# The last tile of a fused decoder layer: raw rows turned and scaled later, the residuals brought in by TensorE, and two pieces of work moved in the queues

## The chip, the cores and the metric

The kernel runs on 1 core of a Trainium2 chip. The metric is the device time of one execution in microseconds. The kernel before has a median of 396.46 us over 3 runs (395.39 to 398.01). The engines are named as the profile names them: PE is TensorE (PEld its weight loads), DVE is VectorE, ACT is ScalarE, POOL is GpSimd, SP is SyncE, which issues loads.

## What is computed

A decoder layer with the norm behind each residual, on x of 8 sequences of 128 tokens, 512 wide, in float32:

```python
x = _layernorm(x + _L0_attn_ref(x, ...))       # rmsnorm, mamba2, residual; rmsnorm, gated MLP 512-1792-512, residual
x = _layernorm(x + _L0_xattn_ref(x, ctx_4096)) # softmax(x ctx^T) ctx, ctx of 128 keys per sequence
x = _layernorm(x + _L0_ffn_ref(x, ...))        # x W_up^T + a rank-8 update of the one expert of 4 with the highest logit
```

where `_layernorm` subtracts the mean and divides by sqrt(var + 1e-5), over the 512 values of a row, without weights. The expert is `argmax(x gate_w^T + expert_bias)`.

## The kernel before

Everything is written out by hand, engine by engine, with counting semaphores: each engine runs its block in order, and `wait_ge(s, n)` halts all behind it on that engine. A tile is one sequence: 128 tokens on the partitions, 512 values along the row. A product of fp32 accuracy is made of three fp32r products (`three_pass`, lines 656 to 658): high by low, high by high, low by high parts, so each operand needs a high part (a copy with rounding, mostly ScalarE) and a low part (a subtraction, VectorE or GpSimd).

The program has three stages. First the mamba2 block (0 to about 132 us): input projections in the order of `IN_ORDER`, whose products `in_proj(n)` feed convolutions and, from n = 14 on, the gate z; `decays_of(b)` builds the exponents of sequence b (two kinds of bf16 products) and then transposes x and the steps of sequence b into bank 5. For b >= 1 these transposes wait for `xb_ok` of sequence b - 1, since bank 5 is one for all: ScalarE's `decay(b - 1)` copies it out (line 1147). `decays_after` says behind which projections the first two stand. Second, gate and up projections (to about 265 us), partly as Strassen products; at their end the down weights and the base weights (W_up with the gate and LoRA columns) are loaded by SP, rounded by ScalarE (`wd_high`, `bw_high`, line 1322) and their low parts made by VectorE and GpSimd.

Third, the tiles (265 us to the end). A tile t passes: `down(t)`, 14 blocks of 128 of the hidden layer, three products each into bank 0 or 1, cut into segments (`SEGS`, for the last tile `END_SEGS`) between which other tiles' pieces stand; `add_mlp` (VectorE: bank + rows, the residual), `moments(0)`, `rstd(0)` (ScalarE: log, then exp), `normed(0)`; `turn_x1` (four transposes), `copy_q`, `attend` (scores against `keyT`, loaded), `row_max`, `exp_scores`, `turn_ex`, `mix` (weights by `key`, loaded), `add_attention`, `moments(1)`, `rstd(1)`, `normed(1)`; `turn_x2`, `copy_x2` and `low_x2` (high and low part of x2), `base` (side 1 holds half of the columns with the logits and LoRA columns, 292 wide; side 0 the other 256), `choose` and `routed` (VectorE: eight small steps from logits to the masked LoRA values; line 1801 is the first, 1825 the last), `turn_z`, `copy_z`, `lora`; `add_ffn` (bank + x2, the residual, line 1842), `moments(2)`, `rstd(2)`, `normed(2)`, `store`. The moments are bn_stats and bn_aggr (lines 1789 and 1791), rstd is lines 1378 and 1380, normed is line 1796.

The tiles are staggered: while `down(t)` runs, tile t - 1 has its attention and tile t - 2 its base, with t - 3 finishing (`tail`, in a loop over pairs of tiles). For the last three tiles the order is written out on each engine behind the loop (`last = 7`); x1 and x2 of tile 7 are turned in two halves (`turn_halves`, `copy_halves`, `low_halves`). SP loads `keyT` and `key` of tile t into the place of its hidden rows once these are split. `store` is a DMA issued from ScalarE's queue, line 1384.

## Time and profile before

| | |
|---|---|
| median of 3 runs | 396.46 us (395.39 to 398.01) |
| the profiled execution | 396.79 us |
| its span, first to last instruction | 395.0 us |
| PE busy | 382.7 us, 97% |
| DVE, ACT, POOL busy | 285.1, 192.5, 152.6 us |
| mean granted PE clock | 0.996 |
| DMA, mean | 65 GB/s |

Idle time is given with what ended it. Matmuls overlap in the rows of the timeline: a row of 0.39 us can begin 0.23 us after the one before. The chain that ended last follows the work back from the last instruction and shows each step without that overlap.

### The profile page before, as it was taken

What the parts mean: (1) busy time and instruction counts of PE and PEld (TensorE: products, weight loads), DVE (VectorE), ACT (ScalarE), POOL (GpSimd) and SP (SyncE); (2) the same over time, 40 slices, a digit from 0 to 9 for tenths busy, and PEclk for the clock granted to TensorE, in tenths of its full rate; (3) what the DMA queues carried; (4) which work ended last, traced back from release to release, by engine and by line L of the source; (5) the groups of instructions that cost most, each with busy time, mean ns of one, the idle gap of its engine ahead of it and who ended that gap; (6) DMA issues with size and microseconds to landing.
All of it is one profiled execution on the core that took longest, in us unless ns stands there. A gap on an engine that the chain in (4) does not pass through costs nothing.

```text
span 395.0 us, 5385 instructions
## 1 busy us (share of the span) xinstructions
PE 382.7 (97%) x1926; PEld 311.5 (79%) x1926; DVE 285.1 (72%) x504; ACT 192.5 (49%) x388; POOL 152.6 (39%) x139
## 2 busy tenths in 40 slices
PE   7999998999999999999999999999999999999983
PEld 3878886766688998888888888887788888897863
DVE  4599981267764987979797979695666756676575
ACT  5868766876757644252424243863324144142241
POOL 6406425844599742738282837850000000000000
PEclk9999999999999999999999999999999999999998
DMA  8901110110001033120212111352110120101002
GB/s 268 319 2 54 55 53 0 54 55 0 2 0 53 3 83 133 53 78 31 95 22 95 52 56 53 124 162 87 55 54 28 54 81 27 53 29 51 27 2 80
DMA packets 11659, 25.52 MB, mean 65 GB/s; under 512 B 1681, under 2 KB 1809, under 8 KB 11634
## 3 DMA queue, kind: packets, MB, share of 16 engines
q1 hardware_dynamic: 10480, 23.10, 18.3%
q10 hardware_dynamic: 1154, 2.10, 1.4%
q8 instruction: 14, 0.23, 0.3%
q14 instruction: 11, 0.09, 0.1%
HBM read 23.10 MB, written 2.10 MB: 64 GB/s over the span
## 4 chain that ended last, share of the span: by engine, by line
PE 71%; DVE 15%; POOL 5%; issue 3%; ACT 3%; DMA 1%; SPq 0%; DVEq 0%; ACTq 0%
PE bank_first L656 8%; PE bank_first L658 8%; PE bank_first L657 8%; PE bank L656 7%; PE bank L657 7%; PE bank L658 7%; DVE big L1546 5%; PE bank_last L656 5%; PE bank_last L657 5%; PE bank_last L658 5%; PE bank L923 2%; PE bank L934 2%; PE bank_last L727 2%; POOL rows L545 1%; PE bank_last L736 1%
## 5 line engine op out<-in xcount | busy, mean ns | idle before, releaser
L656 PE MATMUL bank_first<-sets,station 128*128 128x512 f32 (+1 forms) x172 | 69.9, 406 | 0.1
L656 PE MATMUL bank<-sets,station 128*128 128x512 f32 (+1 forms) x180 | 67.5, 375 | 0.3 <-POOL station L488 0.3
L657 PE MATMUL bank<-sets,station 128*128 128x512 f32 (+1 forms) x180 | 66.1, 367 | 0.0
L658 PE MATMUL bank<-sets,station 128*128 128x512 f32 (+1 forms) x180 | 66.0, 367 | 0.0
L658 PE MATMUL bank_first<-sets,station 128*128 128x512 f32 (+1 forms) x172 | 65.6, 381 | 0.0
L657 PE MATMUL bank_first<-sets,station 128*128 128x512 f32 (+1 forms) x172 | 65.4, 380 | 0.0
L656 PEld LDWEIGHTS bank<-sets,station 128*128 128x128 f32 x180 | 34.3, 190 | 6.8 <-POOL station L488 0.7
L656 PEld LDWEIGHTS bank_first<-sets,station 128*128 128x128 f32 x172 | 32.4, 189 | 8.4 <-issue 2.8
L657 PEld LDWEIGHTS bank<-sets,station 128*128 128x128 f32 x180 | 34.3, 190 | 5.8 <-issue 0.5
L658 PEld LDWEIGHTS bank<-sets,station 128*128 128x128 f32 x180 | 34.2, 190 | 5.5
L657 PEld LDWEIGHTS bank_first<-sets,station 128*128 128x128 f32 x172 | 32.4, 188 | 6.8 <-issue 1.7
L658 PEld LDWEIGHTS bank_first<-sets,station 128*128 128x128 f32 x172 | 32.3, 188 | 6.4
L608 POOL TENSOR_TENSOR big<-tmp,side_f 128x512 f32<-128x512 f32 x17 | 26.5, 1573 | 24.7 <-DVE side_f L1672 24.7
L1378 ACT ACTIVATE small<-small 128x1 f32<-128x1 f32 x24 | 7.1, 295 | 45.7 <-DVE small L1791 45.7
L656 PE MATMUL bank_last<-sets,station 128*128 128x512 f32 (+1 forms) x76 | 28.0, 368 | 0.0
L658 PE MATMUL bank_last<-sets,station 128*128 128x512 f32 (+1 forms) x76 | 27.9, 367 | 0.0
L657 PE MATMUL bank_last<-sets,station 128*128 128x512 f32 (+1 forms) x76 | 27.9, 367 | 0.0
L488 POOL TENSOR_TENSOR station<-raw,station 128x1024 fp32r<-128x1024 f32 x7 | 16.7, 2390 | 26.7 <-ACT station L1056 26.7
L1656 DVE TENSOR_TENSOR station<-raw,station 128x512 fp32r<-128x512 f32 (+1 forms) x24 | 19.0, 832 | 6.1 <-ACT station L1281 6.1
L1281 ACT ACTIVATE station<-raw 128x512 fp32r<-128x512 f32 x12 | 7.5, 625 | 29.8 <-PE bank L658 17.9
L1666 DVE TENSOR_TENSOR station<-side_f,station 128x512 fp32r<-128x512 f32 x24 | 19.5, 814 | 2.1 <-ACT station L1289 2.1
L1546 DVE SCALAR_TENSOR_TENSOR big<-bank,cw,big 128x508 f32<-128x508 f32 (+2 forms) x27 | 19.7, 738 | 0.9 <-ACT big L1129 0.3
(250 smaller groups left out, 867.4 us busy)
## 6 DMA issues: line engine op xcount, KB each, us to landing
raw<-wstream SPq DMA_DIRECT2D x31, 512.0 KB, 3.7
rows<-x SPq DMA_DIRECT2D x8, 256.0 KB, 5.1
big<-ctxT SPq DMA_DIRECT2D x8, 256.0 KB, 2.6
big<-ctx SPq DMA_DIRECT2D x8, 256.0 KB, 3.0
out<-tmp ACTq DMA_DIRECT2D x8, 256.0 KB, 2.0
big<-ln_w SPq DMA_DIRECT2D x1, 256.0 KB, 5.9
big<-lora_b SPq DMA_DIRECT2D x3, 64.0 KB, 5.6
ga<-gate_lora SPq DMA_DIRECT2D x1, 72.0 KB, 5.8
```

Source lines behind the costliest of these rows:

```text
L488: pool.tensor_tensor(dst, raw[:, raw_slot(n), :], hi.bitcast(F32), ALU.subtract).then_inc(w_lo, 1)
L608: pool.tensor_tensor(hid_block(m, hf), blocks(sg[:, k, :]), blocks(value), ALU.mult).then_inc(up_ok, 1)
L656: pe.matmul(ps, a_hi, b_lo, start=first, stop=False)
L657: pe.matmul(ps, a_hi, b_hi, start=False, stop=False)
L658: return pe.matmul(ps, a_lo, b_hi, start=False, stop=last)
L727: pe.matmul(bank[6][:, :], bT[:, tok(b)], cT[:, :, tok(b)], start=True, stop=True).then_inc(s1_done, 1)
L923: mm = pe.matmul(bank[4][:, 0:P], qT[:, bass.ts(c, P)], blocks(keyT)[:, c, :], start=(c == 0), stop=(c == DC - 1))
L934: pe.matmul(bank[5][:, :], exT, key, start=True, stop=True).then_inc(pv_ps, 1)
L1281: act.activation(groupS[:, buf, 0, 0:D], raw[:, raw_slot(n), 0:D], ACT.Copy).then_inc(g_hi, 1)
L1546: v.scalar_tensor_tensor(out=dst[:, :, s:L], in0=src[:, :, 0:L - s], scalar=cw[:, m, 3 - s:4 - s], in1=dst[:, :, s:L], op0=ALU.mult, op1=A ...
L1656: v.tensor_tensor(groupS[:, buf, 1, lo:hi], src, groupS[:, buf, 0, lo:hi].bitcast(F32), ALU.subtract) \
L1666: v.tensor_tensor(groupS[:, buf, 1, q], sums[:, bass.ts(k, D)], groupS[:, buf, 0, q].bitcast(F32), ALU.subtract).then_inc(g_lo, 1)
```

## The change

1. `decays_of(1)` stands one projection later on PE (`decays_after`).
2. GpSimd adds the identity to the four diagonal blocks of the base weights before they are rounded, so that base products contain x2 itself. `add_ffn` goes away for all tiles: moments and norm of the third layernorm read the PSUM banks. It also makes an fp32r identity and the high and low part of tile 7's rows; PE adds two products of these to tile 7's down sum (`add_rows`), so `add_mlp(7)` goes away.
3. For tile 7, ScalarE subtracts the mean of each key row from the key (`center_key`), PE turns it (`turn_key`), ScalarE copies it (`copy_keyT`); the load of `keyT` of tile 7 goes away. With centred keys the mean of x1 adds nothing to the scores that differs between keys, so the raw row is turned (`copy_raw`, `turn_halves`) and 1/std enters as the scale of the exponential (`raw_row_max`, `exp_raw_scores`). Mixing with centred keys shifts a row by a constant, which the next layernorm takes out.
4. x2 of tile 7 is turned before its norm as well: logits are scaled in `choose` (`scale=`), and the last rstd takes the scale in (`rstd_raw`, `rstd_scaled`).
5. The order behind the loop is new: base and lora of tile 5 stand in the middle of the last down projection, those of tile 6 around tile 7's attention, in other banks. Banks are named in four pairs, in the same places.

PE around the second `decays_of` (L710, L712 and L720, L721 are its rows, the rows of L656 to L658 are projections). Before:

```order
L658 MATMUL bank<-sets,station 128x512
L710 MATMUL bank_first<-big,identb 128x512 [waits rows_ok]
L712 MATMUL bank_first<-cs_56,tmp 128x128 x4
L720 MATMUL bank<-ident,big 128x128 [waits xb_ok,cv_done]
L721 MATMUL bank<-ident,big 128x128
L656 MATMUL bank_last<-sets,station 128x512 [waits z_done,hT_lo,w_lo]
L657 MATMUL bank_last<-sets,station 128x512
```

After (710, 712, 720, 721 are 730, 732, 740, 741 there, and 656 to 658 are 676 to 678):

```order
L677 MATMUL bank_last<-sets,station 128x512
L678 MATMUL bank_last<-sets,station 128x512
L730 MATMUL bank_first<-big,identb 128x512 [waits rows_ok]
L732 MATMUL bank_first<-cs_56,tmp 128x128 x4
L740 MATMUL bank_third<-ident,big 128x128 [waits xb_ok,cv_done]
L741 MATMUL bank_third<-ident,big 128x128
L676 MATMUL bank_second<-sets,station 128x512 [waits z_done,hT_lo,w_lo]
```

The decays now stand behind the projection into bank_last.

PE around the turned exponential and the mix of tile 7 (L929 and L934 before, L968 and L973 after). Before:

```order
L929 MATMUL bank<-ident,tmp 128x128 [waits ex_ok]
L656 MATMUL bank_first<-side,rawS 128x292 [waits x2_lo]
L657 MATMUL bank_first<-side,rawS 128x292
L658 MATMUL bank_first<-side,rawS 128x292
L934 MATMUL bank<-big,tmp 128x512 [waits exT_ok]
L656 MATMUL bank_first<-side,rawS 128x292
L657 MATMUL bank_first<-side,rawS 128x292
L658 MATMUL bank_first<-side,rawS 128x292
```

After:

```order
L968 MATMUL bank_third<-ident,tmp 128x128 [waits ex_ok]
L676 MATMUL bank_second<-side,rawS 128x256
L677 MATMUL bank_second<-side,rawS 128x256
L678 MATMUL bank_second<-side,rawS 128x256
L973 MATMUL bank_third<-big,tmp 128x512 [waits exT_ok]
L676 MATMUL bank_second<-side,rawS 128x256
L677 MATMUL bank_second<-side,rawS 128x256
L678 MATMUL bank_second<-side,rawS 128x256
L676 MATMUL bank_second<-side,rawS 128x256
L677 MATMUL bank_second<-side,rawS 128x256
L678 MATMUL bank_second<-side,rawS 128x256
L948 MATMUL bank_first<-ident,tmp 128x128 [waits ln2_u]
```

Before, one chunk of tile 6's base stands ahead of the mix and seven behind it; after, six stand ahead of it (the last two of them shown) and two behind, with the first transposes of the raw x2 (L948) next.

VectorE from tile 7's attention residual on. Before (L1866 is the residual, L1789, L1791 and L1796 moments and norm, L1801 to L1825 the routing of tile 6, L1842 would follow):

```order
L1866 SCALAR_TENSOR_TENSOR tmp<-bank,small,tmp 128x512 [waits pv_ps,rinv_ok]
L1789 BN_STATS tmp<-tmp 128x6 [waits ln2_u]
L1791 BN_AGGR small<-tmp 128x2 [waits ln2_st]
L1801 TENSOR_TENSOR tmp<-bank_first,eb 128x4 [waits route_ps]
L1803 TENSOR_REDUCE small<-tmp 128x1 [waits lg_step]
L1805 SCALAR_TENSOR_TENSOR tmp<-tmp,small,codes 128x4 [waits lg_step]
L1796 TENSOR_SCALAR tmp<-tmp,small 128x512 [waits ln2_rs]
L1811 TENSOR_REDUCE small<-tmp 128x1 [waits lg_step]
L1813 TENSOR_SCALAR tmp<-tmp,small 128x4 [waits lg_step]
L1817 TENSOR_TENSOR tmp<-bank_first,tmp 128x32 [waits lg_step]
L1822 CAST tmp<-tmp 128x2x32 [waits z_step]
L1825 TENSOR_TENSOR tmp<-tmp 128x32 [waits z_step]
```

After (L2000 is the residual in halves, L1924 to L1938 the rest of tile 6's routing, L1958 the low halves, L1887 the moments of tile 7):

```order
L2000 SCALAR_TENSOR_TENSOR tmp<-bank_third,small,tmp 128x256 [waits ln1_out,pv_ps,rinv_ok]
L2000 SCALAR_TENSOR_TENSOR tmp<-bank_third,small,tmp 128x256
L1924 TENSOR_REDUCE small<-tmp 128x1 [waits lg_step]
L1926 TENSOR_SCALAR tmp<-tmp,small 128x4 [waits lg_step]
L1930 TENSOR_TENSOR tmp<-bank_second,tmp 128x32 [waits lg_step]
L1935 CAST tmp<-tmp 128x2x32 [waits z_step]
L1938 TENSOR_TENSOR tmp<-tmp 128x32 [waits z_step]
L1958 TENSOR_TENSOR rawS<-bank_first,rawS 128x256 [waits x2_hi] x2
L1887 BN_STATS tmp<-tmp 128x6 [waits ln2_u]
L1889 BN_AGGR small<-tmp 128x2 [waits ln2_st]
L1903 TENSOR_SCALAR tmp<-bank_last,small 128x512 [waits ln3_rs,stored]
L1913 SCALAR_TENSOR_TENSOR tmp<-bank_third,small,eb 128x4 [waits ln2_rs,route_ps]
```

The routing's last five steps now stand between the residual and the low halves, and the norm of tile 7 is gone from between them.

ScalarE at the store of tile 5 (DMA; L1378 and L1380 before, L1462 and L1464 after are rstd(1) of tile 7). Before:

```order
L1378 ACTIVATE small<-small 128x1 [waits ln2_mv]
L1380 ACTIVATE small<-small 128x1 [waits ln2_log]
L1398 ACTIVATE rawS<-bank 128x256 [waits x2_ps] x2
L1409 ACTIVATE zmT<-bank 96x128 [waits zmT_ps]
L1384 DMA out<-tmp 128x512 [waits ln3_out]
L1409 ACTIVATE zmT<-bank 96x128 [waits zmT_ps]
L1378 ACTIVATE small<-small 128x1 [waits ln3_mv]
L1380 ACTIVATE small<-small 128x1 [waits ln3_log]
```

After:

```order
L1493 ACTIVATE rawS<-bank_first 128x256 [waits x2_ps] x2
L1504 ACTIVATE zmT<-bank_first 96x128 [waits zmT_ps]
L1479 DMA out<-tmp 128x512 [waits ln3_out]
L1462 ACTIVATE small<-small 128x1 [waits ln2_mv]
L1464 ACTIVATE small<-small 128x1 [waits ln2_log]
L1465 ACTIVATE small<-small 128x1
L1466 ACTIVATE small<-small 128x1
```

That rstd stood ahead of the copies of x2 and of the store; it now stands behind the store.

The diff, cut to what the prediction speaks of:

```diff
-END_SEGS = ((0, 8), (8, 9), (9, 10), (10, 11), (11, 14))
+END_SEGS = ((0, 8), (8, 9), (9, 10), (10, 11), (11, 13), (13, 14))
...
+                if t < B - 1:
+                    sp.dma_start(keyT, ctxT[t]).then_inc(ctx_in[t % 2], 16)
...
+            for c in range(DC):
+                n = base_load(c // 2)
+                pool.wait_ge(raw_in[raw_slot(n)], landed(n))
+                diagonal = raw[:, raw_slot(n), bass.ds((c % 2) * D + c * P, P)]
+                pool.tensor_tensor(diagonal, diagonal, ident[:, :], ALU.add).then_inc(eye_ok, 1)
+            pool.wait_ge(wd_lo, NM // 2 - len(POOL_WD))
+            pool.wait_ge(bw_lo, 2)
+            pool.wait_ge(hx_ok, B)
+            pool.tensor_copy(identS, ident[:, :]).then_inc(eye_ok, 1)
+            pool.tensor_copy(rowsS[:, 0, :], rows[:, B - 1, :]).then_inc(eye_ok, 1)
+            pool.wait_ge(eye_ok, DC + 2)
+            pool.tensor_tensor(rowsS[:, 1, :], rows[:, B - 1, :], rowsS[:, 0, :].bitcast(F32), ALU.subtract).then_inc(eye_ok, 1)
...
-            decays_after = {N_DVE_IP + 3: 0, N_DVE_IP + 4: 1}
+            decays_after = {N_DVE_IP + 3: 0, N_DVE_IP + 5: 1}
...
+            def add_rows():
+                pe.wait_ge(eye_ok, DC + 3)
+                for part in range(2):
+                    pe.matmul(bank[1][:, :], identS, rowsS[:, part, :], start=False, stop=False)
+            def turn_key():
+                pe.wait_ge(key_ok, 2)
+                pe.wait_ge(ln_u[0], B - 1)
+                _, key = context(B - 1)
                 for c in range(DC):
+                    mm = pe.transpose(bank[0][:, bass.ts(c, P)], key[:, bass.ts(c, P)], ident[:, :])
+                mm.then_inc(key_ok, 1)
...
+            add_rows()
+            turn_key()
             turn_x1(last - 1)
             turn_x2(last - 2, 1)
             down(last, 1, 1, False, END_SEGS)
...
             turn_ex(last - 1)
             down(last, 1, 3, False, END_SEGS)
             mix(last - 1)
-            down(last, 1, 4, False, END_SEGS)
             base(last - 2, 1)
             base(last - 2, 0)
             turn_x2(last - 1, 0)
-            turn_halves(last, u1, ln_out[0], (2, 0), q_ps)
+            down(last, 1, 4, False, END_SEGS)
+            pe.wait_ge(ln_u[1], last)
+            turn_z(last - 2, bk=5)
+            down(last, 1, 5, False, END_SEGS)
+            lora(last - 2)
+            base(last - 1, 1, range(1), pair=2)
+            turn_halves(u1, ln_u[0], B, (0, 2), q_ps)
+            base(last - 1, 1, range(1, 2), pair=2)
             attend(last, 1, halves=True)
-            turn_z(last - 2, bk=1)
-            lora(last - 2)
+            base(last - 1, 1, range(2, DC), pair=2)
+            base(last - 1, 0, range(1), pair=2)
             turn_ex(last)
-            base(last - 1, 1, range(1), pair=0)
+            base(last - 1, 0, range(1, 2), pair=2)
             mix(last)
-            base(last - 1, 1, range(1, DC), pair=0)
-            base(last - 1, 0, pair=0)
-            turn_halves(last, u2[:, 1, :], ln_out[1], (3, 5), x2_ps)
-            turn_z(last - 1)
-            base(last, 1, range(2), halves=True, free=last - 1)
-            lora(last - 1, pair=0)
-            base(last, 1, range(2, DC), halves=True)
-            base(last, 0)
-            turn_z(last)
-            lora(last)
+            base(last - 1, 0, range(2, DC), pair=2)
+            turn_halves(u2[:, 1, :], ln_u[1], B, (0, 1), x2_ps)
+            base(last, 1, range(2), pair=4, halves=True)
+            turn_z(last - 1, bk=0)
+            base(last, 1, range(2, DC), pair=4, halves=True)
+            lora(last - 1, pair=2)
+            base(last, 0, pair=4)
+            turn_z(last, bk=1)
+            lora(last, pair=4)
...
+                act.wait_ge(eye_ok, 2 * (i + 1))
...
+            def center_key():
+                act.wait_ge(ctx_in[1], 16 * (B - 1))
+                _, key = context(B - 1)
+                act.activation(x1_last, key, ACT.Copy, scale=-1.0 / D, accum_out=key_mean).then_inc(key_ok, 1)
+                act.wait_ge(key_ok, 1)
+                act.activation(key, key, ACT.Identity, bias=key_mean, scale=1.0).then_inc(key_ok, 1)
...
+            def copy_raw():
+                act.wait_ge(down_ps, B)
+                act.wait_ge(ln_u[1], B - 1)
+                for i in range(2):
+                    q = bass.ts(i, 2 * P)
+                    act.activation(u1[:, q], bank[1][:, q], ACT.Copy).then_inc(ln_u[0], 1)
...
+            def rstd_raw(t):
+                act.wait_ge(ln_mv[1], t + 1)
+                act.activation(log2_last, mv[:, 1, 1:2], ACT.Ln, bias=epsc[:, :]).then_inc(ln_log[1], 1)
+                act.wait_ge(ln_log[1], t + 1)
+                act.activation(lrs[:, 1:2], log2_last, ACT.Exp, scale=-0.5).then_inc(ln_rs[1], 1)
+                act.activation(half2_last, log2_last, ACT.Copy, scale=-0.5).then_inc(ln_rs[1], 1)
+                act.activation(r2sq_last, log2_last, ACT.Exp, scale=-1.0).then_inc(ln_rs[1], 1)
+            def rstd_scaled(t, slot):
+                r = lrs[:, slot:slot + 1]
+                act.wait_ge(ln_mv[2], t + 1)
+                act.wait_ge(ln_rs[1], t + 3)
+                act.activation(r, mv[:, slot, 1:2], ACT.Ln, bias=epsc[:, :], scale=r2sq_last).then_inc(ln_log[2], 1)
+                act.wait_ge(ln_log[2], t + 1)
+                act.activation(r, r, ACT.Exp, bias=half2_last, scale=-0.5).then_inc(ln_rs[2], 1)
...
+            center_key()
             copy_q(last - 1)
             copy_x2(last - 2)
             store(last - 3)
             exp_scores(last - 1)
             rstd(1, last - 1)
+            copy_keyT()
+            copy_x2(last - 1)
+            copy_z(last - 2, bk=5)
+            copy_raw()
+            copy_halves(last, qT, q_ps, (0, 2), q_ok)
             rstd(0, last)
-            copy_halves(last, qT, q_ps, (2, 0), q_ok)
-            copy_x2(last - 1)
-            copy_z(last - 2, bk=1)
-            exp_scores(last)
+            exp_raw_scores(last)
             rstd(2, last - 2)
-            rstd(1, last)
-            copy_halves(last, x2S[:, 0, :], x2_ps, (3, 5), x2_hi)
-            copy_z(last - 1)
+            copy_halves(last, x2S[:, 0, :], x2_ps, (0, 1), x2_hi)
+            copy_z(last - 1, bk=0)
             store(last - 2)
-            copy_z(last)
+            rstd_raw(last)
+            copy_z(last, bk=1)
             rstd(2, last - 1)
-            rstd(2, last, slot=0)
+            rstd_scaled(last, 0)
             store(last - 1, u1)
             store(last, u_last)
...
+            def ffn_normed(t, u=u3, pair=6, slot=None, stored_tiles=None):
+                normed(2, t, in_two(u), slot, src=pairs[pair // 2][:, :, 0:D // 2])
+            def normed(i, t, u, slot=None, src=None):
                 k = i if slot is None else slot
                 v.wait_ge(ln_rs[i], t + 1)
-                v.tensor_scalar(u, u, mv[:, k, 0:1], lrs[:, k:k + 1], ALU.subtract, ALU.mult).then_inc(ln_out[i], 1)
+                v.tensor_scalar(u, u if src is None else src, mv[:, k, 0:1], lrs[:, k:k + 1], ALU.subtract, ALU.mult).then_inc(ln_out[i], 1)
...
+            def raw_row_max(t):
+                v.wait_ge(sc_ps, t + 1)
+                v.tensor_reduce(sm[:, 0:1], bank[4][:, 0:P], AX.X, ALU.max, negate=True).then_inc(mx_ok, 1)
+                v.wait_ge(mx_ok, t + 1)
+                v.wait_ge(ln_rs[0], t + 1)
+                v.tensor_tensor(bias_last, sm[:, 0:1], lrs[:, 0:1], ALU.mult).then_inc(mx_ok, 1)
+            def add_attention_halves(t):
+                v.wait_ge(ex_ok, t + 1)
+                v.reciprocal(sm[:, 2:3], sm[:, 1:2]).then_inc(rinv_ok, 1)
+                v.wait_ge(rinv_ok, t + 1)
+                v.wait_ge(pv_ps, t + 1)
+                v.wait_ge(ln_out[0], t + 1)
+                for i in range(2):
+                    q = bass.ts(i, 2 * P)
+                    v.scalar_tensor_tensor(out=u2[:, 1, q], in0=bank[5][:, q], scalar=sm[:, 2:3], in1=x1_last[:, q],
+                                           op0=ALU.mult, op1=ALU.add).then_inc(ln_u[1], 1)
...
-            add_mlp(last, 1)
-            moments(0, last, u1)
+            choose(last - 2)
             normed(1, last - 1, u2[:, 0, :])
-            normed(0, last, u1)
-            route(last - 2)
-            row_max(last)
+            routed(last - 2)
             low_x2(last - 1)
-            add_ffn(last - 2, 1, stored_tiles=last - 2)
-            moments(2, last - 2, u3)
-            add_attention(last, 1)
-            moments(1, last, u2[:, 1, :])
-            choose(last - 1, bk=1)
-            normed(1, last, u2[:, 1, :])
-            routed(last - 1, bk=1)
+            raw_moments(last)
+            ffn_moments(last - 2)
+            raw_row_max(last)
+            normed(0, last, x1_last, src=u1)
+            choose(last - 1, bk=3)
+            add_attention_halves(last)
+            routed(last - 1, bk=3)
             low_halves(last)
-            add_ffn(last - 1, 0, u=u1, pair=0)
-            normed(2, last - 2, u3)
-            route(last)
-            moments(2, last - 1, u1)
-            add_ffn(last, 1, u=u_last)
-            moments(2, last, u_last, slot=0)
-            normed(2, last - 1, u1)
-            normed(2, last, u_last, slot=0)
+            moments(1, last, u2[:, 1, :], value=B + 1)
+            ffn_normed(last - 2, stored_tiles=last - 2)
+            choose(last, bk=5, scale=lrs[:, 1:2])
+            routed(last, bk=5)
+            ffn_moments(last - 1, pair=2)
+            ffn_moments(last, pair=4, slot=0)
+            ffn_normed(last - 1, u=u1, pair=2)
+            ffn_normed(last, u=u_last, pair=4, slot=0)
```

## Rows read from the trace of the kernel before

**Rows 1.** Busy us (xcount) by stretch: PE, PEld, DVE, ACT, POOL; clock, DMA, GB/s

```profile
383.00:395.00 12.00, 5.29 (x34) 4.26 (x34) 7.37 (x23) 2.20 (x8) 0.00 (x0) 0.87 0.17 66
sum 395.00, PE 382.68 PEld 311.46 DVE 285.10 ACT 192.53 POOL 152.61; mean PE 38.27 PEld 31.15 DVE 28.51 ACT 19.25 POOL 15.26
```

**Rows 2.** Waits of TensorE, whole span: who waited for whom, us, times, longest

```profile
PE bank L720 <- ACT big L1147: 1.2, 1, 1.2
```

**Rows 3.** Timeline, 66 to 110 us: start, us, engine, line, op, names, count, [idle before]

```profile
66.69 0.39 PE L712 MATMUL bank_first<-cs,tmp 128*128 128x128 bf16 x4
...
68.30 0.30 PE L720 MATMUL bank<-ident,big 128*128 128x128 f32 x1 [1.22 <-ACT big L1147]
...
67.85 0.31 ACT L1147 ACTIVATE big<-bank 128x164 f32<-128x164 f32 x1
...
109.28 1.30 POOL L541 TENSOR_TENSOR big<-big 128x512 f32<-128x512 f32 x1 [2.57 <-DVE big L1582]
```

**Rows 4.** Timeline, 261 to 274 us: base weights, and tile 0's first norm

```profile
261.97 1.24 POOL L635 CAST side<-ga 128x144 fp32r<-128x144 f32 x1 [1.17 <-DVE big L1678]
263.29 0.55 POOL L637 TENSOR_TENSOR side<-ga,side 128x144 fp32r<-128x144 f32 x1
...
264.80 1.04 ACT L1322 ACTIVATE side<-raw 128x1024 fp32r<-128x1024 f32 x1
266.78 1.07 ACT L1322 ACTIVATE side<-raw 128x1024 fp32r<-128x1024 f32 x1 [0.94 <-DMA raw<-wstream]
...
272.40 0.55 DVE L1796 TENSOR_SCALAR tmp<-tmp,small 128x512 f32<-128x512 f32 x1 [0.60 <-ACT small L1380]
...
273.70 0.60 PE L905 MATMUL bank<-ident,tmp 128*128 128x128 f32 x4
```

**Rows 5.** Timeline, 128 us: GpSimd and VectorE side by side

```profile
128.56 2.40 POOL L563 TENSOR_TENSOR sets<-sets_f,sets 128x1024 fp32r<-128x1024 f32 x1
...
128.71 2.80 DVE L1625 SCALAR_TENSOR_TENSOR tmp<-tmp,rst,big 128x512 f32<-128x512 f32 x1 [3.01 <-POOL rows L545]
```

**Rows 6.** Chain that ended last, 359 to 373 us: start, us, what

```profile
359.14 0.23 PE bank_first L656
...
364.61 0.44 PE bank L905 x4
...
366.17 0.91 PE bank L923 x8
...
368.97 0.86 PE bank L934 x2
...
372.32 0.14 PE bank_last L656
```

**Rows 7.** Timeline, 363 us to the end: the last tile's chain

```profile
363.57 0.29 ACT L1378 ACTIVATE small<-small 128x1 f32<-128x1 f32 x1 [1.01 <-DVE small L1791]
...
378.11 0.33 PE L929 MATMUL bank<-ident,tmp 128*128 128x128 f32 x1
...
378.81 1.13 PE L934 MATMUL bank<-big,tmp 128*128 128x512 f32 x2
...
380.04 0.75 DVE L1866 SCALAR_TENSOR_TENSOR tmp<-bank,small,tmp 128x512 f32<-128x512 f32 x1
...
383.82 0.76 DVE L1853 TENSOR_TENSOR rawS<-bank,rawS 128x256 fp32r<-128x256 f32 x2
...
386.72 0.15 DVE L1801 TENSOR_TENSOR tmp<-bank_last,eb 128x4 f32<-128x4 f32 x1
...
388.27 0.19 DVE L1825 TENSOR_TENSOR tmp<-tmp 128x32 fp32r<-128x32 f32 x1
...
389.75 0.69 DVE L1842 TENSOR_TENSOR tmp<-bank_last,tmp 128x512 f32<-128x512 f32 x1 [0.46 <-PE bank_last L970]
...
391.98 0.55 DVE L1796 TENSOR_SCALAR tmp<-tmp,small 128x512 f32<-128x512 f32 x1 [0.17 <-ACT small L1380]
...
386.84 0.35 ACTq L1384 DMA_DIRECT2D out<-tmp  x1
```

92 lines of the change are left out of this document (60 added, 32 removed).

## The prediction

> **What bounds the kernel now.** I read the page first, then the busy times by stretch. TensorE is busy 382.68 us of 395.00 [rows 1], so only its waits and its queue's contents can move the time; VectorE and ScalarE matter where they keep TensorE waiting, and after its last product. In the list of waits TensorE's longest is 1.2 us, one time, at L720, on ScalarE's L1147 [rows 2]. Then the timeline, at the two places. Around 68 us TensorE has the decays of sequence 1 in its queue, and their transposes need xb_ok, which ScalarE gives only after a table load and the copy at 67.85 [rows 3]. From 383 to 395 us TensorE is busy 5.29 of 12.00 us [rows 1]: there the kernel is a chain of VectorE, ScalarE and short TensorE pieces, and what counts there is VectorE's order.
>
> I write all times on the clock of the trace of before, and subtract the gain of the first edit at the end.
>
> **Edit 1, decays of sequence 1 one projection later.** Before, TensorE ends the row-sum products of the decays at 66.69+0.39 and then stands still 1.22 us until 68.30 [rows 3]. After, the 12 products of the next projection, which before follow the transposes, come first. Twelve products of 0.23 us [rows 6] are 2.8 us, so they run from 66.5 to 69.3, the decays' five bf16 products reach to 69.7 and the transposes start at 69.7: xb_ok has been there since 67.85+0.31 = 68.16. ScalarE comes to the transposed steps later still, behind the exponentials of sequence 0 and two rounding copies of weights. Gain: 1.22 us. Is it kept? What follows is TensorE's own queue until the last VectorE-bound stretch. GpSimd is dense between 109 and 131 us, but its start there waits 2.57 us for VectorE, which follows TensorE [rows 3], so that stretch moves along. I take the whole 1.22; the bounds are 0 (absorbed there) and 1.22.
>
> **Edit 2, identity added to the base weights on GpSimd, rows of tile 7 split.** Four additions of 128x128 come ahead of ScalarE's two copies of the base weights. ScalarE makes these at 264.80 and, released by the DMA, at 266.78 [rows 4]. GpSimd's last work before ends at 263.84 [rows 4]. A 128x128 addition is not in the trace; from a CAST of 128x144, 1.24 us, and the subtraction of the same size, 0.55 us [rows 4], I put it at 0.4 to 1.2. The first pair is then ready by 264.6 to 266.2, the second 0.8 to 2.4 us after 266.78. Behind their readers VectorE has the first tile's residual and moments; its norm is at 272.40 and TensorE turns it at 273.70 [rows 4], so there are 0.75 us of slack (273.70 less 272.95). Behind them GpSimd splits identity and rows: three more pieces, during just these VectorE pieces. What this does is shown at another place: GpSimd's L563 runs from 128.56 for 2.40 us, and VectorE's L1625, started at 128.71, takes 2.80 us [rows 5], where the same operation on the same shape takes 0.75 alone, at 380.04 [rows 7]. It ended only after GpSimd did. The Trainium skill, "GPSIMD Engine Reference", section 1 (Specifications), says that the two engines share their SBUF interfaces, and that a VectorE instruction with two SBUF inputs or in a two-port mode contends; these two rows agree. Cost on TensorE: 0 if the collisions stay inside the 0.75 us; at worst the norm (0.55 us) begins when GpSimd ends. With 0.3 + 1.24 + 2.50 us for the three pieces from 270.9 on (2.50: each as slow as the 2.40 of L563), that is 274.9, the norm ends at 275.5, and TensorE loses 1.8 us. I take 0.3, nearer the lower end, since it needs several collisions in a row to use up the slack. The body of the loop loses one addition of 0.67 to 0.69 us per tile on VectorE (L1842), worth nothing: TensorE is busy there throughout, and VectorE isn't waited for. If the norm out of PSUM were slower, the base products of the next tile would wait for it; they stand behind the down products of a segment and the attention, so I count nothing.
>
> **Edit 3, the last tile.** TensorE first, up to the second product of the attention of tile 7 (mix). From the start of the last down projection at 359.14 its queue holds: 42 products of 0.23 (9.6), two for the rows (0.46), five groups of four transposes of 0.44 (2.2), two attends of 0.91 (1.8), one mix of 0.86, 12 base products of 0.14 and 12 of about 0.12 for tile 5 (3.0; an estimate, 0.14 times 256/292), 12 and 6 for tile 6 (2.3), two lora products and three single transposes (0.6), and the wait for the exponential that it has before (0.4): 21.2 us, ending at 380.4 [rows 6]. From turning the exponential to the mix it is 0.70 us before (378.11 to 378.81), and the two short base products fill only half of it: mix(7) at 380.65, against 378.81 [rows 7], 1.84 us later. I find no wait on ScalarE or VectorE that ends later than TensorE's own queue there. The closest is the centred key: the reciprocal root of tile 4 starts at 363.57 [rows 7], 0.7 earlier without the residual addition, takes 0.5, and two passes over the key of 0.8 and 0.6 (estimates from the 0.55 to 0.75 of whole rows here) end at 364.9, when TensorE comes to it at 365.1.
>
> From there VectorE's order decides. Before: the residual of the attention at 380.04, moments, norm, four transposes, low half of x2 at 383.82 [rows 7], base of tile 7 half a microsecond behind. After: 1.23 us behind the mix, so 381.9; two halves of 0.42 each (an estimate: a little over half of 0.75); then the routing of tile 6, still open, five of the eight small steps that go from 386.72 to 388.46 before, so 1.1 us [rows 7], to 383.85; then the low halves. So base(7) starts when it did: what the raw rows save in front (moments and norm, 1.42 us, and the wait for ScalarE) is spent on the later mix and on the routing. Its side 1 ends at 386.15.
>
> Now the choice of tile 7's expert. It needs ln_rs[1], since x2 was turned raw. VectorE after the low halves (384.6): moments of tile 7 (0.69, 0.18), then the norm of tile 5 out of PSUM, to 386.06. On ScalarE the store of tile 5 stands ahead of rstd_raw and waits for that norm; an issue takes 0.35 us [rows 7]. So rstd_raw starts at 386.4, and the pair of functions with its handovers is 0.60 us [rows 4]: VectorE may choose at 387.05, before it was 386.72 [rows 7]. Loss 0.33, with 0.06 for the scaled add 0.39; nothing if the issue hides (then 0.04).
>
> Behind it: transposed z, its copy, lora: 0.39 later, so VectorE goes on at 390.14 instead of 389.75 [rows 7]. The residual addition of 0.69 [rows 7] is gone: moments at 390.14, ScalarE 0.60 behind, norms from 391.65. The last norm reads PSUM. A tensor_scalar from SBUF takes 0.55, a tensor_tensor from PSUM 0.69 [rows 4, 7]; a tensor_scalar from PSUM is not in the trace, so 0.55 to 0.69; I take 0.68. The Trainium skill, "VectorE: DVE Perf Modes", "Why PSUM operands drop a tier", says that fp32 tensor_scalar runs two elements a cycle only from SBUF; by it the PSUM form has the longer time, and by the SBUF row the end would be 0.14 earlier. So the last norm ends at 392.33; before it is 391.98+0.55 = 392.53 [rows 7]. The two stores behind it keep their 2.5 us to 395.0. Gain of the tail: 0.20. Bounds: issue hidden and norms at 0.55, twice on the path: 0.35+0.28 more, 0.85. A late key, slower halves or transposes: each moves mix(7) and all behind it, down to a loss of 0.5.
>
> **Sum.** 1.22 - 0.3 + 0.2 = 1.1 us off the profiled execution's 396.79 gives 395.7. That execution is 0.33 over the median of 396.46, so I predict **395.4 us**. A change of under 1% (4 us) is about what a measurement of this kernel can't tell from none.
>
> **Rivals.**
> - *Forecast* (1.22 kept, small collision, tail about even): 395.4, chance 0.45.
> - *The tail pays more*: the store's issue hides and the norms cost no more from PSUM. For it: the 0.35 us are the issue's, and nothing in the trace shows how soon a function can start behind one; against: ScalarE's block is in order, and the store waits for the very norm. 0.65 us more, and no collision in edit 2 another 0.3: 394.4. Chance 0.22.
> - *The first edit isn't kept*: GpSimd between 109 and 131 us absorbs it. Against: its 2.57 us wait ahead. Then 1.22 is missing: 396.6. Chance 0.10.
> - *GpSimd holds VectorE at the start of the tiles* (the other side): the place is VectorE's norm at 272.40; the price is 1.8 us at the bound above instead of 0.3, so 396.8, slower than before; it decides from a stall of 1.4 us on TensorE's first transposes of x1, where the two other terms are used up. For it: 2.80 us at 128.71; against: the slack of 0.75 and that the pieces must line up. Chance 0.15. The Trainium skill's line on the shared interfaces ("GPSIMD Engine Reference", section 1) speaks for this one.
> - *Something in the new order waits that I don't see* (two us either way): 0.08.
>
> **How the numbers follow.** The cases reach from 394.4 to 396.8; with the bounds of the tail (0.65 better, 0.7 worse) and some half us for a median of single runs that lie between 395.39 and 398.01, 8 in 10 lie between 393.6 and 397.2. None of the named cases reaches 4 us: faster by over 1% 0.03, within 1% 0.94, slower by over 1% 0.03.
>
> **What would show it.** In the trace after: no wait of TensorE at the decays' transposes near 69 us (edit 1; a wait anywhere in 70 to 135 that is not there now would be where it went). TensorE's first transposes of x1 in tile 0 without a wait: edit 2 hidden; a wait on the norm there, beside a GpSimd cast: the slow rival. The distance from the start of the last down projection to mix(7), 21.5 us; VectorE's low halves right behind the last step of tile 6's routing; the choice of tile 7 waiting for ScalarE rather than for the base products; the last norm 0.68 us. I would be wrong if TensorE waited for the centred key, if the ScalarE functions of the tail brought a table load, or if the halves took as long as whole pieces.

## The result, and the profile after

The changed kernel takes 397.63 us (median of 20 runs, 397.13 to 399.39) where the kernel before takes 396.20 (20 runs, 395.31 to 398.01): a ratio of 1.0034 with a 95% interval of 1.0023 to 1.0045. It is slower by 1.35 us (0.9 to 1.8), where 395.4 was predicted, a gain of 1.1.

TensorE is as busy as before, 382.83 us; its waits have moved. One stretch of the changed kernel (columns as in [rows 1]: window, its length, then TensorE, weight loads, VectorE, ScalarE, GpSimd busy, clock, DMA):

```profile
250.00:275.00 25.00, 23.36 (x104) 18.39 (x103) 20.32 (x22) 14.91 (x17) 18.91 (x14) 1.00 0.43 144
```

TensorE has waits of 1.64 us between 250 and 275, where before it had none that the profile lists, and GpSimd's work there has grown from 11.76 to 18.91 us. In the loop behind it, 275 to 359, TensorE is busy for 84.00 of 84.00 us in both kernels.

The traces differ by up to 2.4 us in when TensorE comes to the first product of the attention of sequence 0 (61.44 to 63.83), so I compare distances between fixed places of the order of work, not times from the start. The places are, in the changed kernel's timeline (start, length, engine, line): the first product of the attention of sequence 0, the turn of the normed rows of sequence 7, the first transposes of x1 of tile 0, and VectorE's last norm.

```profile
62.02 1.02 PE L747 MATMUL bank_last<-big 128*128 128x512 f32 x2
...
130.22 0.66 PE L778 MATMUL bank_last<-ident,tmp 128*128 128x128 f32 x4 [0.52 <-DVE tmp L1723]
...
274.03 0.66 PE L925 MATMUL bank_second<-ident,tmp 128*128 128x128 f32 x4 [1.02 <-DVE tmp L1903]
...
392.63 0.81 DVE L1903 TENSOR_SCALAR tmp<-bank_third,small 128x512 f32<-128x512 f32 x1
```

In the kernel before the first two stand here (the other two are in [rows 4] at 273.70, and the last norm ends at 392.53, of which [rows 7] shows the start):

```profile
62.86 1.02 PE L727 MATMUL bank_last<-big 128*128 128x512 f32 x2
...
131.57 0.66 PE L758 MATMUL bank_last<-ident,tmp 128*128 128x128 f32 x4 [0.52 <-DVE tmp L1625]
```

The differences between these starts, and to the end of the last norm, in us; the same four places in every kernel of this study:

| kernel | start | middle | loop and tail | sum | ratio to before, timed |
|---|---|---|---|---|---|
| before | 68.71 | 142.13 | 118.83 | 329.67 | 1 |
| changed | 68.20 | 143.81 | 119.41 | 331.42 | 1.0034 [1.0023, 1.0045] |
| changed, again | 68.18 | 143.82 | 119.40 | 331.40 | 1.0041 [1.0028, 1.0054] |
| b_decay | 67.94 | 142.14 | 118.90 | 328.98 | 0.9983 [0.9974, 0.9992] |
| b_hold | 67.82 | 142.12 | 118.93 | 328.87 | 0.9982 [0.9969, 0.9994] |
| a_noadd | 68.20 | 142.10 | 119.31 | 329.61 | 1.0006 [0.9993, 1.0020] |
| a_late | 68.20 | 142.10 | 119.29 | 329.59 | 0.9999 [0.9987, 1.0011] |
| a_pair | 67.96 | 143.19 | 119.31 | 330.46 | 1.0019 [1.0001, 1.0038] |
| a_half | 68.21 | 143.42 | 119.39 | 331.02 | 1.0054 [1.0033, 1.0074] |
| a_store | 68.23 | 143.81 | 118.58 | 330.62 | 1.0034 [1.0021, 1.0047] |
| a_late_store | 68.21 | 142.10 | 118.47 | 328.78 | 0.9973 [0.9962, 0.9983] |
| a_best | 67.58 | 142.10 | 118.46 | 328.14 | 0.9971 [0.9957, 0.9986] |

So the three edits gave -0.51, +1.68 and +0.58 us, +1.75 in all, where -1.22, +0.3 and -0.2 had been predicted. The distances repeat to 0.03 us between the two profiled executions of the changed kernel. The start, though, has two outcomes 0.24 us apart in kernels with the same edits (68.20 and 67.96; 67.82 and 67.58); b_hold's section shows them. The timed intervals reach 0.4 to 0.8 us to either side, so a smaller step rests on the traces.

**Start.** The wait in the decays [rows 3] is gone: TensorE's L732, L740 and the product behind them follow each other. But 11 us later there is a new one. GpSimd, VectorE and TensorE in the changed kernel's timeline:

```profile
68.59 0.39 PE L732 MATMUL bank_first<-cs,tmp 128*128 128x128 bf16 x4
68.82 0.28 PE L740 MATMUL bank_third<-ident,big 128*128 128x128 f32 x1
...
76.96 2.37 POOL L495 TENSOR_TENSOR station<-raw,station 128x1024 fp32r<-128x1024 f32 x1
78.20 1.68 DVE L1694 TENSOR_TENSOR station<-tmp,station 128x512 fp32r<-128x512 f32 x1 [1.02 <-ACT station L1203]
80.02 0.47 PE L676 MATMUL bank_second<-side,station 128*128 128x512 f32 x1 [0.52 <-DVE station L1694]
```

In the kernel before, the same two subtractions did not meet:

```profile
77.84 2.36 POOL L488 TENSOR_TENSOR station<-raw,station 128x1024 fp32r<-128x1024 f32 x1
80.41 0.69 DVE L1596 TENSOR_TENSOR station<-tmp,station 128x512 fp32r<-128x512 f32 x1 [1.02 <-ACT station L1156]
```

Once the wait is gone, VectorE comes to it while GpSimd still has its 128x1024 subtraction, and takes 1.68 us for what takes 0.69: TensorE waits 0.52 for it.

**Middle.** The four identity adds, one by one, and what VectorE and ScalarE did beside them, in the changed kernel's timeline:

```profile
262.44 1.44 POOL L651 TENSOR_TENSOR raw<-raw,ident 128x128 f32<-128x128 f32 x1
263.84 1.44 POOL L651 TENSOR_TENSOR raw<-raw,ident 128x128 f32<-128x128 f32 x1
265.24 2.23 POOL L651 TENSOR_TENSOR raw<-raw,ident 128x128 f32<-128x128 f32 x1
267.43 1.44 POOL L651 TENSOR_TENSOR raw<-raw,ident 128x128 f32<-128x128 f32 x1
...
262.05 1.52 DVE L1781 TENSOR_TENSOR sets<-raw,sets 128x1024 fp32r<-128x1024 f32 x1
263.49 1.47 DVE L1781 TENSOR_TENSOR sets<-raw,sets 128x1024 fp32r<-128x1024 f32 x1
264.88 2.28 DVE L1881 TENSOR_TENSOR station<-big,station 128x1792 fp32r<-128x1792 f32 x1
267.08 1.47 DVE L1787 TENSOR_TENSOR side<-raw,side 128x1024 fp32r<-128x1024 f32 x1
...
265.37 1.06 ACT L1370 ACTIVATE side<-raw 128x1024 fp32r<-128x1024 f32 x1 [1.83 <-POOL raw L651]
268.96 1.06 ACT L1370 ACTIVATE side<-raw 128x1024 fp32r<-128x1024 f32 x1 [2.53 <-POOL raw L651]
```

In the kernel before, VectorE's same instructions stood there without an add beside them:

```profile
263.41 2.65 DVE L1683 TENSOR_TENSOR sets<-raw,sets 128x1024 fp32r<-128x1024 f32 x2
265.98 2.01 DVE L1783 TENSOR_TENSOR station<-big,station 128x1792 fp32r<-128x1792 f32 x1
```

Each add lasts almost as long as the VectorE instruction beside it: 1.44 beside 1.47 to 1.52, 2.23 beside 2.28. ScalarE's second copy of the base weights, at 266.78 before [rows 4], starts at 268.96, though by the second of the places above (130.22 for 131.57) the kernel is 1.35 us ahead there: 3.5 us late. TensorE pays twice: here, for a VectorE that is itself slower (2.28 us for 2.01), and at the first transposes of x1 (274.03 above, 1.02 us) for the norm behind the late copy.

```profile
267.31 0.47 PE L676 MATMUL bank_first<-sets,station 128*128 128x512 f32 x1 [0.62 <-DVE station L1881]
```

**Tail.** From the second product of tile 7's attention to the end, in the changed kernel's timeline:

```profile
381.47 1.12 PE L973 MATMUL bank_third<-big,tmp 128*128 128x512 f32 x2
382.69 0.88 DVE L2000 SCALAR_TENSOR_TENSOR tmp<-bank_third,small,tmp 128x256 f32<-128x256 f32 x2 [1.50 <-issue]
384.49 0.75 DVE L1958 TENSOR_TENSOR rawS<-bank_first,rawS 128x256 fp32r<-128x256 f32 x2
...
385.98 0.80 DVE L1903 TENSOR_SCALAR tmp<-bank_last,small 128x512 f32<-128x512 f32 x1
386.81 0.35 ACTq L1479 DMA_DIRECT2D out<-tmp  x1
387.20 0.29 ACT L1462 ACTIVATE small<-small 128x1 f32<-128x1 f32 x1 [0.75 <-DVE tmp L1903]
387.83 0.22 DVE L1913 SCALAR_TENSOR_TENSOR tmp<-bank_third,small,eb 128x4 f32<-128x4 f32 x1 [1.06 <-ACT small L1465]
...
389.69 0.33 PE L1004 MATMUL bank_first<-ident,tmp 128*128 128x128 f32 x1 [1.08 <-DVE tmp L1938]
...
391.88 0.39 ACT L1473 ACTIVATE small<-small 128x1 f32<-128x1 f32 x1 [0.85 <-DVE small L1889]
```

It is the chain that the prediction drew: VectorE norms tile 5 out of PSUM, only then does ScalarE issue the store, only then does it take the logarithm for tile 7 (387.20), and VectorE, with nothing else to do for 1.06 us, waits to choose tile 7's expert.

### The profile page after: what moved, and what is told of

Same layout as the page of the kernel before. It is cut to its first block and busy times, and to the rows that moved or that the text cites. A ratio compares the mean times of both kernels' runs of the same rounds, so it can differ in the third digit from the quotient of the medians.

```text
span 395.9 us, 5408 instructions
## 1 busy us (share of the span) xinstructions
PE 382.8 (97%) x1928; PEld 311.2 (79%) x1932; DVE 282.7 (71%) x497; ACT 195.8 (49%) x396; POOL 161.4 (41%) x146
## 5 line engine op out<-in xcount | busy, mean ns | idle before, releaser
L676 PE MATMUL bank_second<-sets,station 128*128 128x512 f32 (+1 forms) x96 | 35.6, 370 | 0.0
L678 PE MATMUL bank_second<-sets,station 128*128 128x512 f32 (+1 forms) x96 | 34.8, 363 | 0.0
L677 PE MATMUL bank_second<-sets,station 128*128 128x512 f32 (+1 forms) x96 | 34.8, 363 | 0.0
L676 PE MATMUL bank_third<-sets,station 128*128 128x512 f32 (+1 forms) x84 | 31.7, 378 | 0.4 <-POOL station L495 0.4
L678 PE MATMUL bank_third<-sets,station 128*128 128x512 f32 (+1 forms) x84 | 31.0, 369 | 0.0
L677 PE MATMUL bank_third<-sets,station 128*128 128x512 f32 (+1 forms) x84 | 31.0, 369 | 0.0
L676 PEld LDWEIGHTS bank_second<-sets,station 128*128 128x128 f32 x96 | 18.1, 189 | 3.4 <-issue 0.5
```

Of the source, the lines that this page charges most:

```text
L676: pe.matmul(ps, a_hi, b_lo, start=first, stop=False)
L677: pe.matmul(ps, a_hi, b_hi, start=False, stop=False)
L678: return pe.matmul(ps, a_lo, b_hi, start=False, stop=last)
```

## Experiments

The theories after the result: (1) the middle's loss is the four adds, each held by a VectorE instruction; (2) rivals to it: an add of this size costs 1.4 us by itself, or its rate by the element is lower beside VectorE; (3) the tail's loss is the store ahead of ScalarE's three steps; (4) the first edit, alone, keeps its 1.2 us.

**b_decay: the first edit alone.** On the kernel before:

```diff
-            decays_after = {N_DVE_IP + 3: 0, N_DVE_IP + 4: 1}
+            decays_after = {N_DVE_IP + 3: 0, N_DVE_IP + 5: 1}
```

> The kernel before with the decays of sequence 1 one input product later and nothing else. Theory (edit 1 is kept and the other two edits cost): 1.2 us faster than before, near 395.0, with TensorE free of the 1.22 us wait at 68.3 and every later instruction about 1.3 us earlier. Rival (the gain of edit 1 is given back where GpSimd and VectorE meet, whatever the identity adds do): between 0 and 0.4 us faster, TensorE busy in 250 to 275 as little as in the changed kernel (23.4 of 25).

0.9983 of before, 0.7 us; by the trace 0.69 (0.77 at the start). That is neither theory's number. Two of TensorE's waits from 61 to 131 us say where the rest went:

```profile
PE bank L656 <- DVE station L1596: 0.5, 1, 0.5
PE bank L656 <- POOL station L488: 0.2, 1, 0.2
```

The second stands in the kernel before too (0.31 us there); the first is new and is the 0.5 that comes off 1.22. Theory 4 falls.

**b_hold: keep the two subtractions apart.** b_decay, and on GpSimd:

```diff
+            pool.wait_ge(y_lo, 1)
             lo_part(GU_CHUNK, ringS[:, 0, 1, :], ringS[:, 0, 0, :])
```

> The kernel before with the decays of sequence 1 later, and with one wait more: GpSimd's subtraction for the first loop weight (128x1024, 2.36 us at 76.91) starts only when VectorE's subtraction for y of sequence 0 is done. Theory (edit 1 loses 0.5 us at 80 because these two instructions now overlap and VectorE's takes 1.67 us instead of 0.69): VectorE's takes 0.69 again, TensorE's wait of 0.52 at 80 is gone, and the kernel is 1.0 to 1.3 us faster than before, near 394.5 where before has 395.75. Rival (TensorE would wait at 80 anyway, for ScalarE or for the chain of sequence 1): the time of edit 1 alone, 0.5 to 0.8 us faster than before, with a wait of 0.3 or more left near 80.

VectorE's subtraction takes 0.69 us again and the wait at 80 is gone, so the overlap was its cause. The time doesn't tell what that is worth: 0.9982 against b_decay's 0.9983, with intervals of 0.4 us and more to either side. By the table the start gains only 0.12 us on b_decay, but that pair isn't like with like. About 117 us in, VectorE and GpSimd come to their next instructions together, and one of them is held. Here are the changed kernel and then a_pair, whose program is the same up to there:

```profile
116.60 0.74 DVE L1723 SCALAR_TENSOR_TENSOR tmp<-tmp,rst,big 128x512 f32<-128x512 f32 x1
116.64 1.30 POOL L561 TENSOR_TENSOR sets_f<-sets_f 128x256 f32<-128x256 f32 x1
...
117.66 1.33 DVE L1724 SCALAR_TENSOR_TENSOR tmp<-tmp,rst,big 128x512 f32<-128x512 f32 x1
117.70 0.74 POOL L561 TENSOR_TENSOR sets_f<-sets_f 128x256 f32<-128x256 f32 x1
```

Where GpSimd is held, TensorE's next wait for it is 0.43 us (at 123.25); where VectorE is held, 0.19 us (at 124.05), and the start is 0.24 us shorter. VectorE is held in the traces of before, b_decay, a_pair and a_best, GpSimd in the other eight; what decides it isn't shown. Like with like, b_hold's wait gains 0.38 us (67.82 against the changed kernel's 68.20) and again 0.36 (a_best's 67.58 against b_decay's 67.94), out of 0.52. Most of the rest goes 42 us later, where TensorE now waits 0.51 us for GpSimd instead of 0.43:

```profile
122.36 0.39 PE L657 MATMUL bank<-sets,station 128*128 128x256 f32 x1 [0.51 <-POOL station L488]
```

That is GpSimd's dense stretch behind 109 us, named in a rival of the prediction. So that rival was right for a few tenths: 0.52 of the 1.22 goes at 80 us, a place that it had not named, and part of what is won back there is lost in the stretch that it had.

**a_noadd: the changed kernel without the four adds.**

```diff
-                pool.tensor_tensor(diagonal, diagonal, ident[:, :], ALU.add).then_inc(eye_ok, 1)
+            pool.sem_inc(eye_ok, DC)
```

(The loop around the add goes too, and with it the third layernorm's residual is left out of what the kernel computes.)

> The changed kernel without the four GpSimd adds that put the identity onto the diagonal blocks of the base weights; so the residual of the third norm is left out of what it computes. Theory 1 (the 1.8 us lost between 250 and 275 is these adds, 1.4 us each ahead of ScalarE's base copies and beside VectorE's long instructions): 1.6 to 1.9 us faster than the changed kernel, near 395.9; ScalarE's two base copies then start near 263.5 and 265.5 instead of 265.4 and 269.0. Rival (the loss is in the rows and identity splits, the longer GpSimd stream or the bank layout): less than 0.5 us faster than the changed kernel, near 397.3.

The middle falls from 143.81 to 142.10 us, 0.03 under before, with the identity and row splits still in place; the time is 1.0006 of before, against 1.0034 and 1.0041. The whole loss of the middle comes from the adds. ScalarE's two copies start at 263.01 and 264.56.

**a_late: the same adds, behind VectorE's first norm.** The four adds and the copies' waits for them are taken out of their old place, and behind GpSimd's other waits stands:

```diff
+            pool.wait_ge(ln_out[0], 1)
+            for c, diagonal, _ in diagonals():
+                pool.tensor_tensor(diagonal, diagonal, ident[:, :], ALU.add).then_inc(eye_ok, 1)
+            for c, diagonal, high in diagonals():
+                pool.wait_ge(eye_ok, c + 1)
+                pool.tensor_copy(high, diagonal).then_inc(eye_ok, 1)
+            for c, diagonal, high in diagonals():
+                pool.wait_ge(eye_ok, DC + c + 1)
+                pool.tensor_tensor(baseS[:, 1, c, bass.ts(c, P)], diagonal, high.bitcast(F32), ALU.subtract) \
+                    .then_inc(eye_ok, 1)
```

TensorE's first base product waits for all twelve.

> The changed kernel with the four identity adds moved behind the base copies and behind VectorE's first norm: GpSimd adds the identity to the raw diagonal blocks, and makes their high and low parts anew (4 adds, 4 copies, 4 subtractions of 128x128) while VectorE waits for TensorE. Nothing waits for it before the first use of the base weights, near 287. Theory 1 (an add is slow only beside VectorE's two-operand instructions): an add takes 0.3 to 0.5 us here instead of 1.44, all twelve are over within 6 us, and the time is that of the kernel without the adds, near 395.9. Rival 2 (an add of this size takes 1.4 us by itself on GpSimd): adds of 1.4 us here as well, the twelve take about 12 us or more, over just at or after TensorE's first base product, with a wait there of 0 to 3 us and a time of 396 to 399.

Middle 142.10, time 0.9999 of before: the whole loss is gone, with eight instructions more on GpSimd. Groups by line (duration in ns: least, median, most), and one of the subtractions with what VectorE did:

```profile
L658 POOL TENSOR_TENSOR raw<-raw,ident x4: 447/452/459, 273.6 to 274.9; 128x128 f32<-128x128 f32 x4
...
277.48 2.23 POOL L664 TENSOR_TENSOR side<-raw,side 128x128 fp32r<-128x128 f32 x1
277.26 2.13 DVE L1893 TENSOR_TENSOR station<-big,station 128x1792 fp32r<-128x1792 f32 x1
```

Alone an add takes 0.45 us, so rival 2 in its first form falls. The same kernel shows both prices for one kind of instruction: three of its four subtractions take 0.45 us, the fourth, beside VectorE's 128x1792, takes 2.23. ScalarE and TensorE were at work beside the four adds too (ScalarE on its 128x1792 from 272.74 for 1.69 us); VectorE was idle from the end of its norm at 273.42. No wait of TensorE is left between 250 and 300 us.

**a_pair and a_half: the same elements in two instructions, or in eight.**

```diff
+                pair = raw[:, raw_slot(n), :].rearrange("p (c q) -> p c q", q=P)[:, 2 * i::DC + 1, :]
+                pool.tensor_tensor(pair, pair, ident[:, :].unsqueeze(1).broadcast_to([P, 2, P]), ALU.add) \
+                    .then_inc(eye_ok, 2)
```

> The changed kernel with its four identity adds of 128x128 made two of 128x2x128, the same elements in half as many instructions. Theory 1a (beside VectorE's long two-operand instructions a GpSimd instruction lasts as long as VectorE's, whatever its own size): about 1.44 and 1.4 to 2.3 us for the two, 3 to 4 us in all instead of 6.4; ScalarE's second base copy starts near 267 instead of 269, and 1.0 to 1.8 us of the loss in the middle come back. Theory 1b (it runs at a lower rate by the element): 2.9 and 3.6 us, 6.4 in all as before, and the time of the changed kernel.

```diff
+                for hf in range(2):
+                    half_ = bass.ts(hf, P // 2)
+                    pool.tensor_tensor(diagonal[:, half_], diagonal[:, half_], ident[:, half_], ALU.add).then_inc(eye_ok, 1)
```

> The changed kernel with its four identity adds of 128x128 made eight of 128x64, the same elements in twice as many instructions. Theory 1a (an instruction of GpSimd lasts as long as VectorE's beside it, whatever its own size): each takes 1.2 to 2.3 us while VectorE is busy with two operands, 8 us or more in all, ScalarE's second base copy starts 1.5 us or more later, and the kernel is 1 to 3 us slower than the changed kernel. Theory 1b (a lower rate by the element): 0.7 to 0.8 us each, 6.4 in all, and the time of the changed kernel to within 0.4 us.

a_pair's two adds, of twice the width, and then a_half's first four of eight, of half the width, with two of VectorE's instructions beside them:

```profile
263.23 1.72 POOL L651 TENSOR_TENSOR raw<-raw,ident 128x256 f32<-128x256 f32 x1
265.69 0.93 POOL L651 TENSOR_TENSOR raw<-raw,ident 128x256 f32<-128x256 f32 x1 [0.75 <-DMA raw<-wstream]
```

```profile
261.87 1.30 POOL L653 TENSOR_TENSOR raw<-raw,ident 128x64 f32<-128x64 f32 x1
263.13 1.30 POOL L653 TENSOR_TENSOR raw<-raw,ident 128x64 f32<-128x64 f32 x1
264.39 2.10 POOL L653 TENSOR_TENSOR raw<-raw,ident 128x64 f32<-128x64 f32 x1
266.45 0.32 POOL L653 TENSOR_TENSOR raw<-raw,ident 128x64 f32<-128x64 f32 x1
...
262.92 1.34 DVE L1783 TENSOR_TENSOR sets<-raw,sets 128x1024 fp32r<-128x1024 f32 x1
264.18 2.14 DVE L1883 TENSOR_TENSOR station<-big,station 128x1792 fp32r<-128x1792 f32 x1
```

Beside a VectorE instruction of 128x1024, adds of 64, 128 and 256 columns take 1.30, 1.44 and 1.72 us: four times the elements, 0.42 us more. A lower rate by the element (1b) would have given 0.72, 1.44 and 2.88; it falls. The rows fit engines that take turns: an add waits for the VectorE instruction under way, and the next VectorE instruction waits for the add (1.47 us beside 128 columns, 1.34 beside 64, 1.22 without one, the changed kernel's L1787 at 270.06).

My forecast of a_half was wrong all the same, in its total: 6.02 us for the eight, not 8 or more. It had assumed that VectorE would always have a next instruction. After three it had to wait for ScalarE's base copy, which waited for the adds, and the last five adds ran at 0.32 us. a_half's distances are 0.4 us under the changed kernel's; its timed ratio is the highest of all, 1.0054, with an interval that overlaps those of the changed kernel. Its ten runs fall into two groups, 396.5 to 397.5 and 398.7 to 399.7 us, and the trace is of the lower one, so whether and why it is slower stays open. a_pair's second copy starts at 266.71, as expected. Its two adds took 2.65 us in all, under the 3 to 4 of the forecast: the second, 0.75 us late for want of its load, took 0.93. But the middle got back only 0.62 us, not 1.0 to 1.8: the wide adds slow VectorE more (2.55 us for its 128x1792, against 2.28), and TensorE waits 0.91 us for that one (0.62 in the changed kernel). The wait for the norm, 1.02 us, is gone.

**a_store: ScalarE's steps ahead of the store.**

```diff
-            store(last - 2)
             rstd_raw(last)
+            store(last - 2)
             copy_z(last, bk=1)
```

> The changed kernel with ScalarE's three steps for the last second norm put ahead of the store of tile 5 instead of behind it; nothing else. Theory 3 (the store, which waits for the norm of tile 5 out of PSUM, 0.80 us, holds ScalarE and with it the routing of tile 7): routing starts about 1.0 us earlier, TensorE's turn of z of tile 7 follows its base products with a wait of under 0.2 us instead of 1.08, and the time is 0.7 to 1.0 us below the changed kernel, near 396.8. Rival (the tail is set by the norms of tiles 6 and 7 on VectorE, or by lora of tile 6): less than 0.3 us below it.

In its timeline the steps no longer wait for the norm of tile 5, and the choice comes 0.23 us behind TensorE's last low base product:

```profile
385.97 0.28 ACT L1462 ACTIVATE small<-small 128x1 f32<-128x1 f32 x1
...
386.41 0.35 ACTq L1479 DMA_DIRECT2D out<-tmp  x1
...
386.61 0.22 DVE L1913 SCALAR_TENSOR_TENSOR tmp<-bank_third,small,eb 128x4 f32<-128x4 f32 x1 [0.23 <-PE bank_third L678]
...
388.48 0.33 PE L1004 MATMUL bank_first<-ident,tmp 128*128 128x128 f32 x1 [0.24 <-DVE tmp L1938]
```

The 0.24 us is TensorE's wait for z, just over the 0.2 of the forecast. The tail falls from 119.41 to 118.58 us. The timed ratio did not show it (1.0034, against 1.0034 and 1.0041 for the changed kernel; 0.8 us is 0.0020): two of its eleven runs, at 398.4 and 398.8 us, lift it. Its median is 1.0 us above that of before, where the changed kernel's stood 1.4 and 1.8 above. The next pair settles it.

**a_late_store and a_best.** a_late_store has the edits of a_late and a_store; a_best has b_hold's wait as well. The changed kernel ran once more beside them, as a_again.

> The changed kernel once more, as the yardstick for its variants on one chip. By the traces' sum from the decays of sequence 0 to the end (0.5 gained at the start, 1.8 lost in the middle, 0.45 in the tail) it stands 1.3 to 1.7 us above the kernel before; a rival that the first verdict owed 0.5 us or more to the chip it ran on expects less than 0.9 us.

> The changed kernel with both repairs: the identity added late, and the last second norm's ScalarE steps ahead of the store of tile 5. Theory (the two losses are apart and add up): 0.9 us below the kernel with the late identity alone (which stood at that of before), near 394.9 where before has 395.75; routing of tile 7 within 0.3 us of TensorE's last low base product. Rival (the tail gives the 0.9 back once it starts earlier): the time of before.

> All three repairs: identity late, ScalarE's steps ahead of the store, and GpSimd's subtraction for the first loop weight behind VectorE's for y of sequence 0. Theory (sharing between GpSimd and VectorE costs at both places and apart): 1.3 to 1.6 us below before, near 394.3 where before has 395.75. Rival (the wait put on GpSimd delays its later work on the chain of the sequences): at or above the kernel with two repairs, near 394.9.

The changed kernel repeats: 1.0041, slower by 1.6 us. a_late_store is 0.9973 of before, 1.0 us faster, and 0.0026 under a_late: 1.0 us, where the traces show 0.82 for the store. The two repairs add up. a_best stands 0.6 us lower by its trace, of which 0.24 is the outcome at 117 us, but timed it is the same, 0.9971. a_late_store beats both kernels; that the third repair adds anything isn't shown by time.

## Why the prediction was wrong

**Edit 1: the mechanism was right, the keeping was not.** No wait at the decays, as predicted. The failed step is "Is it kept?": I looked at the GpSimd stretch from 109 on and nowhere in between. Of 1.22 us, 0.51 stayed in the changed kernel and 0.77 in b_decay. Given back were 0.52 at 80 us in both, and in the changed kernel another 0.24 by the outcome at 117 us (a wait for GpSimd of 0.43 us at 123, where b_decay has 0.19 and before 0.31). The test that the prediction itself named, a wait between 70 and 135 that wasn't there, is the one that found it. VectorE's subtraction for y came 0.2 us behind the end of GpSimd's before (80.41, against 77.84+2.36). The edit moved VectorE's by 2.21 us (to 78.20) and GpSimd's by 0.88 (to 76.96), so they meet. Those two rows would have shown how little room there was.

**Edit 2: the term that decided.** I took 0.3 us, and 1.68 came. The size of an add alone was right (0.45 measured, 0.4 to 1.2 estimated), but the upper end was probably a case of what was missed: the CAST of 1.24 us [rows 4] ran beside VectorE's 128x1024 of 1.21 us from 261.83, and a CAST of 128x128 takes 0.29 us in the changed kernel where VectorE reads PSUM (271.41). The failed step is the place where I looked for the collision. I had read [rows 5] as a danger for VectorE at its norm at 272.40, beside GpSimd's later splits; these splits were cheap (1.28 us for the longest). What collided were the adds themselves, earlier, with VectorE's instructions over 128x1024 and 128x1792, which had stood there in the trace of before at 263.41 and 265.98 (shown above). With them the estimate would have been four adds of 1.4 and more, the second pair ready 3.5 us later than the copy at 266.78 [rows 4], and the 0.75 us of slack used up. The prediction had read just this out of [rows 5], that one engine's instruction ends only after the other's (0.75 became 2.80), and did not apply it to the adds.

The slow rival thus had the right outcome and nearly the right price (1.8 against 1.68) for a partly wrong reason: it was VectorE that held GpSimd, and ScalarE's copies carried the delay on. The norm at which it looked was not held: it took 0.55 us from 273.43, beside GpSimd's split of the rows (1.28 us from 272.33). That the price came out is luck. I gave it 0.15 since the pieces would have to line up. They are not independent: four short instructions next to four long ones collide every time.

The Trainium skill, "SBUF — State Buffer", Who interferes with whom, says that a VectorE instruction with two SBUF inputs contends with a GpSimd instruction that reads SBUF; its section SBUF: two separate sides calls the pair of ports that they share an exclusive lock and not a split of bandwidth. These runs agree: 1.30, 1.44 and 1.72 us for 64, 128 and 256 columns. I had cited only the sentence of the Trainium skill's "GPSIMD Engine Reference", section 1 (Specifications), which says that they contend and not how; by the lock, each add costs what is left of VectorE's instruction, plus its own part. The durations fit that: 128 columns take 0.14 us more than 64 beside VectorE and 0.13 us more alone (0.45 and 0.32).

**Edit 3: 0.78 us off, in two terms.** From the first transposes of x1 to tile 7's second attention product it was 107.44 us instead of the predicted 106.95 (380.65 less 273.70): 0.49. Of this, 0.12 is in the loop (85.39 us to the first product of the last down projection, 85.27 before), which I had at nothing. Most of the rest are two waits inside that projection that my queue count left out:

```profile
369.31 0.33 PE L968 MATMUL bank_third<-ident,tmp 128*128 128x128 f32 x1 [0.17 <-ACT tmp L1497]
...
374.21 0.42 PEld L978 LDWEIGHTS bank_second<-ident,tmp 128*128 128x128 f32 x4 [0.18 <-DVE tmp L1903]
```

The first of them is no cost of the change: the kernel before has it too, 0.18 us at 367.94. From the second attention product to the choice of tile 7's expert I had 6.40 us and it took 6.36: halves, routing of tile 6, low halves, norm of tile 5, issue, three steps, in this order. From the choice to the end I had 5.28 and it took 5.61. The scaled reciprocal root took 0.75 from 391.88 to the norm's start, not 0.60, and the norm out of PSUM 0.81, not 0.68. The range that I gave for the norm, 0.55 to 0.69, was not a bound: I had a tensor_tensor from PSUM and a tensor_scalar from SBUF, and the form that is both is slower than either. The Trainium skill, "VectorE: DVE Perf Modes", Why PSUM operands drop a tier, says that an operand in PSUM holds fp32 to the single rate; these runs agree in direction (0.81 us against 0.55).

**The rivals.** "The tail pays more" was wrong: the store's issue does not hide (387.20 follows 386.81+0.35 at once). It was mine to remove: the order of two lines on ScalarE, in a_store, is worth the 0.8 us. "The first edit isn't kept" happened by three fifths in the changed kernel (0.71 of 1.22) and by over a third in b_decay (0.45), mostly at another place than the one it named.

**The sum.** Errors of 0.71, 1.38 and 0.78 us all have one sign. The range was built from the cases one at a time, around a forecast that took all of the 1.22 and the lower end of the collision; three misses of one sign together were outside it. Nor was a change under 1% beyond telling, as I had written: twenty runs of each kernel told this one to 0.45 us.

## What to carry to other kernels

Before placing work on GpSimd, list what VectorE runs in that window: beside its instructions with two SBUF inputs a short GpSimd instruction cost about the length of theirs. Two wide adds lost less than four (1.09 us of the middle against 1.71), eight narrow ones no more than four by their trace (1.32), since VectorE ran out of work; a place where VectorE waits for TensorE lost nothing. When a wait ahead of the chain is removed, look at every pair on the two engines that just missed each other before. And where an engine issues a store that waits for another engine, put what the critical chain needs ahead of it.

## What the hardware showed that I had not expected

- A GpSimd subtraction of 128x128 takes 0.45 us or 2.23 us in one and the same loop, and an add's own size hardly matters: 64, 128 and 256 columns take 1.30, 1.44 and 1.72 us beside 128x1024 on VectorE, and 64 columns 0.32 alone.
- It works both ways: VectorE's 128x512 subtraction took 1.68 us instead of 0.69 when it started 1.24 us into a GpSimd instruction of 2.37.
- Where both engines come to their next instruction within 0.04 us, either may be held (116.60 and 117.66 above), and TensorE's start stretch differs by 0.24 us with it.
- Beside ScalarE's copies and TensorE's products, with VectorE idle, GpSimd's 128x128 adds took 0.45 us.
- A tensor_scalar with two columns as scalars takes 0.78 to 0.81 us out of PSUM and 0.55 out of SBUF, on 128x512; a tensor_tensor with one input in PSUM takes 0.69 (L1842 before, which reads two banks in the same halves).
